# Linear attention scan: keys and weighted queries spread as two rounded parts, outer products kept in PSUM, terms issued later

## What is computed

```python
phi_q = jax.nn.elu(q) + 1.0
phi_k = jax.nn.elu(k) + 1.0
...
def step(carry, xs):
    S, K = carry
    pq, pk, vt, bt, mt = xs
    K = K * bt[..., None] + pk[:, :, None, :]
    S = S * bt[..., None, None] + pk[:, :, None, :, None] * vt[:, :, None, None, :]
    num = jnp.einsum('bhd,bhmdc->bhmc', pq, S)
    den = jnp.einsum('bhd,bhmd->bhm', pq, K) + EPS
    y = jnp.sum(num / den[..., None] * mt[..., None], axis=2)
    return ((S, K), y)
...
y = jnp.moveaxis(ys, 0, 1).reshape(b, t, H) @ Wout.T + bout
z = x + y
# layer norm of z with ln_g, ln_b; the block's result is added to x
```

## Time and profile before

| | us |
|---|---|
| median of 3 runs | 1468.37 |
| lowest and highest run | 1466.29, 1468.88 |
| span of the profiled execution, first to last instruction | 1407.0 |
| difference of the median and the span | 61.4 |
| first matmul of the changed loop | 64.1 |
| last `H` written by it (L758) | 318.6 |
| one turn of the loop (L758 to L758, turns in the middle) | 28.30 |
| PE busy in such a turn | 27.71 |
| DVE busy | 26.18 |
| ACT busy | 9.99 |
| POOL busy | 12.83 |

### The profile page before, as it was taken

One profiled execution on the slowest core, in us unless ns is written; L12 is line 12 of the kernel. 1 busy time (PEld: TensorE's weight loads), 2 busy tenths in 40 slices (PEclk: granted clock), 3 DMA queues, 4 the chain that ended last, 5 costly groups with the idle time before them and its releaser, 6 DMA issues. The chain is left out here.

```text
span 1407.0 us, 26525 instructions
## 1 busy us (share of the span) xinstructions
PE 1211.5 (86%) x7852; PEld 790.4 (56%) x7852; DVE 1044.5 (74%) x2575; ACT 884.2 (63%) x2302; POOL 841.7 (60%) x774
## 2 busy tenths in 40 slices
PE   6879999973777999399689999998978999999797
PEld 3333344422556888234367777774656777777465
DVE  1289999885797998456488888874648888888564
ACT  6623333332444665067489989996648898899674
POOL 0045443514771666331788888886658887788663
PEclk9899999985898999589799999999999999999999
DMA  4800000001321221410000000000000000000001
GB/s 111 288 1 0 1 0 1 1 0 58 106 93 65 71 73 56 161 35 0 23 1 3 2 0 1 0 2 1 1 23 2 2 3 1 1 0 1 1 1 60
DMA packets 35021, 43.99 MB, mean 31 GB/s; under 512 B 5620, under 2 KB 24977, under 8 KB 34912
## 3 DMA queue, kind: packets, MB, share of 16 engines
q1 hardware_dynamic: 30304, 34.27, 7.5%
q0 software_dynamic: 4608, 8.47, 1.9%
HBM read 22.65 MB, written 21.12 MB: 31 GB/s over the span
## 5 line engine op out<-in xcount | busy, mean ns | idle before, releaser
L2099 DVE TENSOR_TENSOR R<-bank,tab 128x1024 f32<-128x1024 f32 x128 | 156.0, 1224 | 70.2 <-ACT sq L2009 69.4
L2043 ACT ACTIVATE W<-W,nm 128x128 f32<-128x128 f32 x512 | 198.3, 393 | 0.4
L1797 POOL TENSOR_TENSOR R<-R 128x512 f32<-128x512 f32 x128 | 161.1, 1280 | 16.0 <-DVE R L2099 16.0
L2122 DVE CUSTOM_DVE_ANT_0 W<-bank,mask_q,rn 128x128 f32<-128x128 f32 x512 | 147.5, 345 | 17.4 <-PE bank L1918 12.8
L1812 POOL TENSOR_TENSOR W<-W,rden 128x512 f32<-128x512 f32 x128 | 132.5, 1040 | 40.6 <-DVE rden L2129 35.2
L1308 POOL DMA_INDIRECT expert_rows<-Yt,xin x80 | 82.6, 1032 | 67.8 <-DVE Yt L1281 49.8
L1011 POOL DMA_INDIRECT expert_slots<-tok_rows,dst x64 | 67.5, 1054 | 66.4 <-ACT tok_rows L1035 45.6
L2043 ACT ACTIVATION_READ_ACCUMULATOR W<-W,nm 128x1 f32 x512 | 98.7, 193 | 0.0
L2027 ACT ACTIVATE QK<-bank 128x512 f32<-128x512 f32 x128 | 75.1, 587 | 35.6 <-PE bank L1893 33.7
L726 DVE TENSOR_TENSOR_SCAN S<-beta,U 128x512 f32<-128x512 f32 x64 | 93.5, 1483 | 0.0
L1943 PE MATMUL bank<-PT,VA 128*64 128x128 f32 (+1 forms) x1024 | 85.8, 261 | 3.7 <-ACT PT L2051 2.8
(11 more groups left out here) (350 smaller groups left out, 3481.2 us busy)
## 6 DMA issues: line engine op xcount, KB each, us to landing
expert_slots<-empty SPq DMA_DIRECT2D x8, 650.0 KB, 6.6
xin<-expert_slots SPq DMA_DIRECT2D x8, 650.0 KB, 4.0
expert_rows<-empty SPq DMA_DIRECT2D x8, 512.0 KB, 6.7
pair_rows<-expert_rows SPq DMA_DIRECT2D x16, 256.0 KB, 4.4
expert_raw<-w1e_dram SPq DMA_DIRECT2D x9, 256.0 KB, 2.9
expert_raw<-w2e_dram SPq DMA_DIRECT2D x9, 256.0 KB, 3.2
tok<-x_dram SPq DMA_DIRECT2D x8, 256.0 KB, 4.7
out_dram<-tok_out SPq DMA_DIRECT2D x8, 256.0 KB, 2.6
```

Source lines behind the costliest of these rows:

```text
L1797: nc.gpsimd.tensor_tensor(halves[:, :, 0, :, z, :], halves[:, :, 0, :, z, :], halves[:, :, 1, :, 1 - z, :], ALU.add).then_inc(summed, 1)
L2043: m = nc.scalar.activation(x, x, ACT.Exp, scale=-1.0, bias=nm[:, p % RING, j:j + 1], accum_out=den[:, p % RING, j:j + 1])
L2099: nc.vector.tensor_tensor(R[:, i, qk, :, :].rearrange("p c (h d) -> p c h d", d=DH), x, y.to_broadcast([P, 2, HEADS, DH]), ALU.mult).then_ ...
L2122: m = nc.vector.tensor_tensor_reduce(W[:, p % RING, j * P:(j + 1) * P], ps[BS[i]][:, cols], k.const["mask_q"][:, cols], rn[:, par, 2 * s + ...
```

## The change

1. Keys and weighted queries are rounded to a high part by ACT (`key_high`, `share_high`) and the rest is made by POOL (`key_low`, `share_low`); the spread matrix is copied once into float32r by DVE. Each spread is now two float32r matmuls, high and low, that accumulate in the bank, in place of one float32 matmul. `divide` writes over `phq_mixed`.
2. `outer` writes its product back into the bank, and the scans read it there. `queries_spread(c, i)` for i below 4 therefore waits for both scans that read bank 3 + i (`s_scan`), not for `outer` alone.
3. On DVE the terms stand later, each behind a scan that frees a bank; on PE `summed` stands between the spreads.
4. The clearing of used semaphores is done in two parts, the first in `combine`, the second in `retention` as before.

```diff
-            U = [buf(f"U{d}") for d in range(D0)]
+            rounded = lambda n, shape: k.sb(n, shape, F32R, ctx)
+            spread = rounded("spread_r", [P, D0, P])
+            phk_parts = [rounded(f"phk_{part}", [P, CH]) for part in ("hi", "lo")]
+            share_parts = [[rounded(f"phq_share_{part}{m}", [P, CH]) for m in range(M0)] for part in ("hi", "lo")]
...
                 def keys_spread(c, d):
-                    pe.wait_ge(phi, 2 * c + 1)
+                    pe.wait_ge(phk_lo, c + 1)
                     if c > 0:
                         pe.wait_ge(t_done, NS * (c - 1) + d + 5)
-                    nc.tensor.matmul(ps[BV + d][:], w["spread"][:, d, :], phk[:], start=True, stop=True).then_inc(u_mm, 1)
+                    for part in range(2):
+                        m = nc.tensor.matmul(ps[BV + d][:], spread[:, d, :], phk_parts[part][:], start=(part == 0), stop=(part == 1))
+                    m.then_inc(u_mm, 1)
...
                 def queries_spread(c, i):
-                    pe.wait_ge(shared, 2 * c + i % 2 + 1)
+                    pe.wait_ge(share_lo, 2 * c + i % 2 + 1)
                     if i < 4:
-                        pe.wait_ge(u_done, 4 * c + i + 1)
+                        pe.wait_ge(s_scan, NS * c + 2 * i + 2)
...
+                def share_high(c, m):
+                    act.wait_ge(shared, 2 * c + m + 1)
...
+                    nc.scalar.activation(share_parts[0][m][:], mixed[m][:], ACT.Copy).then_inc(share_hi, 1)
+
+                def key_high(c):
+                    act.wait_ge(phi, 2 * c + 1)
...
+                    nc.scalar.activation(phk_parts[0][:], phk[:], ACT.Copy).then_inc(phk_hi, 1)
...
                         inverse(c, 1)
+                        share_high(c, 0)
                     if more:
                         keep_values(c + 1)
+                    if now:
+                        share_high(c, 1)
...
                         exponent(c + 1, 1)
+                        key_high(c + 1)
...
+                nc.vector.tensor_copy(spread[:], w["spread"][:]).then_inc(spread_r, 1)
...
-                    nc.vector.tensor_tensor(U[d][:], ps[BV + d][:], vs[c % 2][:], ALU.mult).then_inc(u_done, 1)
+                    nc.vector.tensor_tensor(ps[BV + d][:], ps[BV + d][:], vs[c % 2][:], ALU.mult).then_inc(u_done, 1)
...
-                    nc.vector.tensor_tensor_scan(S[i][:], beta[i % 2][:, chunk(c)], U[i // 2][:], 0.0,
+                    nc.vector.tensor_tensor_scan(S[i][:], beta[i % 2][:, chunk(c)], ps[BV + i // 2][:], 0.0,
...
-                    nc.gpsimd.tensor_tensor(share[m][:], mixed[m][:], lden[m][:], ALU.mult).then_inc(shared, 1)
+                    nc.gpsimd.tensor_tensor(mixed[m][:], mixed[m][:], lden[m][:], ALU.mult).then_inc(shared, 1)
+
+                def share_low(c, m):
+                    pool.wait_ge(share_hi, 2 * c + m + 1)
+                    nc.gpsimd.tensor_tensor(share_parts[1][m][:], mixed[m][:], share_parts[0][m][:].bitcast(F32),
+                                            ALU.subtract).then_inc(share_lo, 1)
+
+                def key_low(c):
+                    pool.wait_ge(phk_hi, c + 1)
+                    nc.gpsimd.tensor_tensor(phk_parts[1][:], phk[:], phk_parts[0][:].bitcast(F32), ALU.subtract).then_inc(phk_lo, 1)
...
                         divide(c, 1)
+                        share_low(c, 0)
+                        share_low(c, 1)
                     if more:
                         rope(c + 1, 0)
                         rope(c + 1, 1)
+                        key_low(c + 1)
```

More of the change, by code:

```diff
@@ L450, in linear_attention @@
             (k_mm, q_mm, v_mm, u_mm, den_mm, p_mm, sum_mm, rot, rope_sum, exped, plus1, phi, v_sb, k_scan, u_done, s_scan,
-             t_done, kp_done, ln_den, rden, shared, mixed_r, eps_set) = map(sem, (
+             t_done, kp_done, ln_den, rden, shared, mixed_r, eps_set, spread_r, phk_hi, phk_lo, share_hi, share_lo) = map(sem, (
                  "k_mm", "q_mm", "v_mm", "u_mm", "den_mm", "p_mm", "sum_mm", "rot", "rope_sum", "exped", "plus1", "phi", "v_sb",
-                 "k_scan", "u_done", "s_scan", "t_done", "kp_done", "ln_den", "rden", "phq_shared", "phq_mixed", "deps_set"))
+                 "k_scan", "u_done", "s_scan", "t_done", "kp_done", "ln_den", "rden", "phq_shared", "phq_mixed", "deps_set",
+                 "spread_made", "phk_hi", "phk_lo", "share_hi", "share_lo"))
             (z_done, squared1, var1, logged1, rstd1, scaled, biased, resid, centred2, squared2, var2, logged2, rstd2,
@@ L506, in queries_spread @@
                 def queries_spread(c, i):
-                    pe.wait_ge(shared, 2 * c + i % 2 + 1)
+                    pe.wait_ge(share_lo, 2 * c + i % 2 + 1)
                     if i < 4:
-                        pe.wait_ge(u_done, 4 * c + i + 1)
+                        pe.wait_ge(s_scan, NS * c + 2 * i + 2)
                     else:
                         pe.wait_ge(t_done, NS * c + i - 3)
-                    nc.tensor.matmul(ps[BV + i % 4][:], w["spread"][:, i // 2, :], share[i % 2][:],
-                                     start=True, stop=True).then_inc(p_mm, 1)
+                    for part in range(2):
+                        m = nc.tensor.matmul(ps[BV + i % 4][:], spread[:, i // 2, :], share_parts[part][i % 2][:],
+                                             start=(part == 0), stop=(part == 1))
+                    m.then_inc(p_mm, 1)
                 def summed(c, i):
@@ L588, in _ @@
                     if now:
+                        summed(c, 0)
                         queries_spread(c, 2)
+                        summed(c, 1)
                         queries_spread(c, 3)
-                        summed(c, 0)
-                        summed(c, 1)
+                        summed(c, 2)
                         queries_spread(c, 4)
                         queries_spread(c, 5)
-                        summed(c, 2)
-                        summed(c, 3)
                     if last:
@@ L600, in _ @@
                         queries_spread(c, 6)
+                        summed(c, 3)
                         queries_spread(c, 7)
@@ L786, in _ @@
                         state(c, 3)
-                        term(c, 0)
-                        term(c, 1)
                         outer(c, 3)
@@ L792, in _ @@
                         rotate(c + 1, 1)
+                    if now:
+                        term(c, 0)
+                        state(c, 5)
+                    if more:
                         features(c + 1, 0)
                     if now:
-                        state(c, 5)
-                        term(c, 2)
+                        term(c, 1)
+                        state(c, 6)
                     if last:
@@ L799, in _ @@
                     if now:
-                        term(c, 3)
+                        term(c, 2)
+                        state(c, 7)
                     if last:
@@ L803, in _ @@
                     if now:
-                        state(c, 6)
+                        term(c, 3)
                         term(c, 4)
                         term(c, 5)
-                        state(c, 7)
                         term(c, 6)
@@ L1327, in _ @@
         def _(pool):
+            nc.gpsimd.sem_clear(range(k.first_spent, k.scan_spent + 1))
             for q in range(0, NCH, 2):
@@ L1482, in _ @@
         def _(pool):
-            nc.gpsimd.sem_clear(range(k.first_spent, k.last_spent + 1))
+            nc.gpsimd.sem_clear(range(k.scan_spent + 1, k.last_spent + 1))
             prepare_split(k, 0, raw[0], pool)
```

11 lines of the change are left out of this document (7 added, 4 removed).

## The result

The changed kernel takes 1510.46 (median of four runs, 1510.14 to 1511.88), and the kernel before, run beside it, 1467.33 (1459.57 to 1468.88). The ratio is 1.0309, interval 1.0283 to 1.0335: slower by 3.1%, or 43 us. The forecast was 1509, with a range of 1480 to 1525.

A forecast was written before the change was run, and what follows sets the result against it. The prediction took PE (27.71 busy) and DVE (26.18) as nearly full in a 28.30 turn, so who waits for whom decides. Laid-out turns +27 and clock +14 gave +41, 1468.4 + 41 = 1509, range 1480 to 1525.

The forecast's parts named there:

- The cost of a spread: On PE, a float32r pair takes 0.47, saving 0.39 per spread, 4.7 a turn: PE from 27.7 to 23.0.
- DVE writing a bank: On DVE, `outer` writing a bank instead of SBUF makes no difference, with bounds of 0 and +0.1 each.
- The contention: Eight of ten DVE scans, reading one bank, run free of POOL: 1.1 saved for S5, 0.5 for S3 each turn.
- The two passages: PE's list waits for POOL's low parts before the query rotation, then for S7; turn 32.6 against 28.3, +4.3.
- The clock: In the loop, PE's pauses drop it to 1.2 GHz in most turns: 2 a turn, bounds 0 and 4, +14 altogether.
- The first two turns and the last two: The two turns up to the loop's first `x_scale` cost +6.9 together, the last two +0.8.
- The frame: Whole execution: profiled 1407.0 becomes 1448; the median lies 61.4 above the span, so 1468.4 + 41 = 1509.
- The sum: Over the whole kernel, +27 from the laid-out turns and +14 from PE's lower clock give +41.
- that the clock holds: Rival: PE's clock in the loop does not fall, longest whole pause being 2.9; only +27, 1495; chance 0.2.
- The dearer lists: Rival: POOL still holds scans (1.1 a turn), or float32/float32r changes cost PE 0.8; 13 more, 1522; chance 0.12.
- the waits did not shrink: Rival: loop waits shrink in part, by quicker POOL subtractions or better-overlapped PE tail; +5 to +20, 1473 to 1488; chance 0.12.
- That DVE becomes the bound: Rival: waits at the rotation and tail are covered, DVE alone binds at 26.2 a turn; -15, 1453; chance 0.09.

The follow-up runs named there:

- e3_front: The changed kernel with the next chunk's query matmuls and z's variance moved on PE ahead of the first two query spreads: 1479.77, ratio 1.0106.
- e5_best: The changed kernel with its instructions kept but reordered on PE and DVE so that neither serial passage is left: 1459.0, ratio 0.9875.
- e7_best_nofront: The better order (e5_best) with query matmuls and z's variance put back behind the first two query spreads: 1490.86, ratio 1.0086.
- e8_front_fill: The queries-first kernel (e3_front) with three unread matmuls added ahead of the fourth query spread: 1479.97, ratio 1.0014.
- e2_fill: The changed kernel with five unread matmuls a turn in PE's pauses, 2 ahead of the query spreads, 3 ahead of the fourth: 1496.2, ratio 1.0228.
- e1_before: The kernel before, unchanged, run and profiled a second time: 1468.4, span 1466.6.
- e4_single: The changed kernel with single float32 spreads again, no roundings or subtractions; products in PSUM and the changed order stay: 1506.98, ratio 1.0287.

## Why the prediction was right, step by step

The turn from 216.10, with times counted from there as the prediction does:

| step | forecast | seen |
|---|---|---|
| division of m = 0 starts | 6.8 | 6.79 |
| division of m = 1 ends | 9.9 | 9.96 |
| POOL's low parts end | 12.4 | 12.42 |
| rotation of the queries | 15.8 | 17.52 |
| end of S7 | 23.7 | 25.47 |
| `router` starts | 28.7 | 32.22 |
| next `x_scale` | 32.6 | 36.07 |

- **The cost of a spread.** Right: a pair of float32r matmuls starts 0.23 apart (216.70, 216.93), and PE's busy time falls to 22.94 where the clock holds. A change between float32 and float32r costs nothing that shows: from `summed` at 246.99 over a pair to `router` at 248.32 it is 1.33, which is 0.86 and 0.47.
- **DVE writing a bank.** Right at the lower bound: two `outer` into banks take 1.27, 0.59 between starts, like its other reads of a bank.
- **The contention.** Right. The scan at 235.42 takes 1.21 while POOL's `qa` runs from 234.99 to 236.25; before, the scan with two SBUF inputs took 2.29 beside the same instruction. All 64 scans of S now last 1.19 to 1.22. `z_scale`, with two SBUF inputs, takes 0.99 beside `phk_lo` and not the 0.74 of before: 0.25, where the forecast had 0.3. The Trainium skill's page "SBUF — State Buffer", section "SBUF: two separate sides", on the port that is wanted only with two SBUF inputs, agrees here with scans too.
- **The two passages.** Right in place and order, and e3_front, e5_best and e7_best_nofront show them as causes: with the first gone the turn is 4.5 shorter, with the new order around the second 4.8, with both 9.25. That order moves several things at once, so the 4.8 are not split by move; the part of the clock in the second passage is 1.6 (e8_front_fill). The price of the first comes from the order of PE's list: three matmuls that depended on nothing late stood behind one that did.
- **The clock.** Right in place, too small in size. The rotation is 1.7 late and the stretch from S7 to `router` takes 6.75 instead of 5.0, and both are largely PE at half clock: the matmuls for the queries start 1.71 apart (230.81 to 232.52), as in the earlier trace rows. Over the 32.6 laid out the five turns are 2.8 longer on average (3.5, 2.7 and 1.8 in the three shown), where I took 2 out of 0 to 4. The windows below show the fall behind the pauses. e2_fill shows that it is the clock: there the rotation is at 15.8, as laid out, and two turns take 32.73.
- **The first two turns and the last two.** Too low: +11.3 instead of +6.9, and +2.1 instead of +0.8. The first turns were laid out without the clock, and the 2 a turn didn't cover them: the wait at the rotation there is 5.68 and 4.77 (at 96.81 and 127.68). If the 27 laid out without the clock hold, 20 of the 46.9 are left for it, where the forecast had 14. e2_fill bears on the first turns: from the loop's first matmul to the first `x_scale` it takes 76.25 there, against 79.03 in the changed kernel and 68.95 in e1_before. So of the 10.1 more, 2.8 went with the pauses filled, and the 7.3 that stay are near the 6.5 laid out (6.9 less the 0.4 of the copy). The other 1.2 of the 11.3 stand ahead of the loop's first matmul, 0.5 of it for the copy.
- **The frame.** This step was wrong: "the median lies 61.4 above its span". The span of an execution is within 2 us of its time (1466.6 and 1468.4, 1510.0 and 1511.88). The 61.4 was most likely the difference between one short execution and the usual ones (the time of the execution first profiled is not on record). It did no harm only because it was carried through as a constant, and because the loop is the same in both profiles.
- **The sum.** That +41 met 43 is in part luck, since two misses nearly cancel: the loop cost 5.9 more, and the stretches behind it gave 3.5 back, which no step had. The latter is within what executions of these stretches differ by (1142.4 to 1147.8 in e1_before to e4_single).

The rivals: that the clock holds fell with the windows. The dearer lists did not come, since no scan is held and a change of form costs nothing, and the waits did not shrink. That DVE becomes the bound came true as a mechanism only in e5_best, where both places were repaired, at 26.0 a turn (26.2 was its forecast) and a ratio of 0.9875 (1453 would be 0.990).

The windows of PE's clock in the turn, from the end of `values` on:

```profile
225.16:229.10 3.94, 1.26 (x5) 0.78 (x5) 3.68 (x5) 1.76 (x4) 3.94 (x4) 1.00 0.00 0
229.10:233.60 4.50, 4.48 (x7) 1.54 (x6) 0.00 (x0) 3.09 (x5) 0.66 (x1) 0.62 0.00 0
233.60:235.56 1.96, 0.00 (x1) 0.00 (x1) 1.94 (x4) 0.00 (x0) 0.57 (x1) 1.00 0.00 0
235.56:239.00 3.44, 3.44 (x6) 1.41 (x6) 3.44 (x5) 1.68 (x3) 1.65 (x2) 0.56 0.00 0
239.00:241.72 2.72, 0.75 (x2) 0.03 (x1) 2.72 (x4) 0.00 (x0) 0.30 (x1) 0.92 0.00 0
241.72:246.60 4.88, 4.88 (x11) 2.90 (x12) 2.52 (x4) 0.00 (x0) 0.00 (x0) 0.65 0.00 0
246.60:252.17 5.57, 5.19 (x22) 3.17 (x20) 1.98 (x3) 2.12 (x4) 2.50 (x2) 1.00 0.00 0
```

Each stretch in which PE was busy 0 to 1.26 still stands at 0.92 to 1.00; the work that follows it runs at 0.56 to 0.65. So a pause is paid for behind itself, by the matmuls that were waited for.

## What to carry to other kernels

When a producer is made longer (here a low part on a third engine), look at what stands behind its consumer in the consumer's list: instructions that depend on nothing late belong ahead of the wait. Work taken from an engine that is full shows as time only if the engine next to it can run on; here the same 4.7 us of saved matmuls lost 1.0 a turn in one order and gained 2.5 in another. And a pause on PE had a second price here, at the clock, which was read by filling it with unread matmuls.

## What the hardware showed that was not expected

- The spans of two executions of the same kernel differ by 60 us of 1467, 52 of them in one stretch (129.8 against 182.3 between the loop and the first row that the experts write back), with the same instructions; the four timed runs of that kernel beside the changed one lie within 9 us. One profile of such a kernel isn't a frame for sums over the whole span.
- Adding 4.3 us of unread work a turn to PE made the kernel faster, 1.0309 to 1.0228, and three unread matmuls a turn 1.0106 to 1.0014.
- The clock fell behind pauses of 2.18 and 0.50 with one short spread between them (1.26 busy of 3.94). In the turn of e5_best shown, with pauses of 1.23 and 1.50 as the longest, it stayed at 1.00.
